# Store order in the start and layernorm of three token chunks inside the last two groups of each cross-attention

## What is computed

```python
def _layernorm(x, axis=-1, eps=1e-05):
    m = jnp.mean(x, axis=axis, keepdims=True)
    v = jnp.var(x, axis=axis, keepdims=True)
    return (x - m) / jnp.sqrt(v + eps)
...
x = x + _L0_xattn_ref(_layernorm(x, axis=-1), ctx_768, ...)
x = x + _L0_ffn_ref(_layernorm(x, axis=-1), ...)
...
x = x + _L3_xattn_ref(_layernorm(x, axis=-1), ctx_768, mask_BxS2_bf1, ...)
x = x + _L3_ffn_ref(_layernorm(x, axis=-1), ...)
```

## Time and profile before

| what | value |
|---|---|
| median of 3 runs | 3842.04 us (3838.91 to 3844.39) |
| profiled execution | 3844.8 us, span 3843.1 us |
| PE busy | 3605.2 us (94%) |
| DVE, ACT, POOL busy | 2533.8, 1933.4, 654.0 us |
| mean granted PE clock | 0.968 of full speed |

### The profile page before, as it was taken

How to read it: one execution, slowest core, us unless ns; L and a number is a source line. 1 busy time by engine, 2 the same in 40 slices (tenths; PEclk the granted TensorE clock), 3 DMA queues, 4 the chain that set the end, 5 groups by cost and what they waited for, 6 DMA issues and landing times. The chain is left out here.

```text
span 3843.1 us, 50411 instructions
## 1 busy us (share of the span) xinstructions
PE 3605.2 (94%) x17554; PEld 1557.4 (41%) x17555; DVE 2533.8 (66%) x5367; ACT 1933.4 (50%) x2358; POOL 654.0 (17%) x946
## 2 busy tenths in 40 slices
PE   5999999799999999987998899999799999998996
PEld 2333333365533333324665333332433333332664
DVE  4888888556678888844223655553478888885523
ACT  2677777621137777772332444445203777777111
POOL 3201000200041000013221301010313001001242
PEclk7999999999999999998999899999899999999998
DMA  6300000123000000015001500000140000001144
GB/s 128 56 19 14 19 14 11 48 76 79 24 26 19 17 16 18 10 37 229 31 30 41 125 18 18 18 18 6 58 94 31 18 18 15 18 11 49 53 121 133
DMA packets 132652, 171.33 MB, mean 45 GB/s; under 512 B 38378, under 2 KB 106588, under 8 KB 130256
## 3 DMA queue, kind: packets, MB, share of 16 engines
q1 hardware_dynamic: 122288, 142.42, 13.4%
q0 software_dynamic: 10144, 26.08, 2.7%
HBM read 131.27 MB, written 40.84 MB: 45 GB/s over the span
## 5 line engine op out<-in xcount | busy, mean ns | idle before, releaser
L1537 DVE TENSOR_REDUCE mx<-ps 128x1 f32<-128x400 f32 (+1 forms) x3584 | 1819.3, 566 | 506.7 <-PE ps L2276 495.4
L1281 ACT ACTIVATE probs<-ps,zero_col 128x1024 f32<-128x1024 f32 (+1 forms) x1040 | 1111.9, 1111 | 579.1 <-PE ps L2315 578.7
L2276 PE MATMUL ps<-k_stack,q_stack 97*128 97x400 bf16 (+1 forms) x3584 | 1077.1, 339 | 50.7 <-DMA k_stack<-k_parts 27.2
L2315 PE MATMUL ps<-q_stack,k_stack 100*128 100x512 bf16 (+2 forms) x3328 | 1056.4, 381 | 6.0 <-ACT probs L1281 6.0
L2329 PE MATMUL ps<-probs,v 128*32 128x512 f32 (+2 forms) x5824 | 892.1, 608 | 0.2 <-ACT probs L1281 0.2
L2276 PEld LDWEIGHTS ps<-k_stack,q_stack 97*128 97x128 bf16 x3584 | 290.7, 97 | 1051.4 <-DVE mx L1537 623.9
L1281 ACT ACTIVATE probs<-ps,mask_col 128x1024 f32<-128x1024 f32 (+1 forms) x416 | 440.0, 1111 | 160.1 <-PE ps L2315 159.9
L2315 PEld LDWEIGHTS ps<-q_stack,k_stack 100*128 100x128 bf16 (+2 forms) x3328 | 323.2, 100 | 344.1 <-ACT probs L1281 65.6
L2329 PEld LDWEIGHTS ps<-probs,v 128*32 128x32 f32 (+2 forms) x5824 | 140.0, 111 | 264.5 <-issue 248.0
L1690 DVE SCALAR_TENSOR_TENSOR x_res<-ps,comb,x_res 128x256 f32<-128x256 f32 x336 | 148.2, 479 | 63.4 <-PE ps L2587 58.2
L1349 ACT ACTIVATE h_t_s<-ps 128x512 f32<-128x512 f32 x80 | 47.8, 597 | 254.6 <-PE ps L2578 254.6
(11 more groups left out here) (298 smaller groups left out, 2770.0 us busy)
## 6 DMA issues: line engine op xcount, KB each, us to landing
q_stack<-q_parts SPq DMA_DIRECT2D x384, 64.0 KB, 2.2
q_parts<-qk_part SPq DMA_DIRECT2D x32, 384.0 KB, 2.5
w_up<-in_up SPq DMA_DIRECT2D x17, 704.0 KB
w_up_s<-in_expert SPq DMA_DIRECT2D x40, 256.0 KB, 2.7
k_stack<-k_parts SPq DMA_DIRECT2D x48, 200.1 KB, 7.4
k_stack<-k_parts POOLq DMA_DIRECT2D x48, 200.1 KB, 4.2
k_parts<-qk_part SPq DMA_DIRECT2D x24, 384.0 KB, 2.9
w_all<-in_up SPq DMA_DIRECT2D x8, 1024.0 KB, 12.6
```

What stands on the lines that cost most here:

```text
L1281: act.activation(PR[pair[0] % 4][0:r, :, :], PS[0:r, 2 * b:2 * b + 2, :], ACT.Exp, bias=mask_col[0:r, k:k + 1] if L == 3 else zero_col[0:r ...
L1537: ins = dve.reduce_max(MX4[g % 2][:, u, c:c + 1], PS[:, bank, 0:CK[c]], AX.X)
L2276: last = mm(PS[:, bank, 0:CK[c]], QS[g][0:97, slot_of(j), qt * P:(qt + 1) * P], KS[0:97, (g * hpg + j) * nsub, CKO[c]:CKO[c] + CK[c]], sta ...
L2315: last = mm(PS[0:r, b + i, :], KS[0:rows, (g * hpg + jj) * nsub + sub, k * P:k * P + r], QS[g][0:rows, slot_of(jj) + sub, :], start=sub == ...
```

## The change

In the start SP's order is another: the second query part is stored right behind the first loads of keys, key parts 4 to 7 are stored between the loads (they stood behind the gate loads), and the second group's keys are loaded last. In every attention's last iteration the `bn_stats` of the first 12 token tiles move from the fourth group to the third, where their variances follow; ACT takes the root of these at the beginning of the fourth group; there DVE inverts at key tile 1 and normalises two token tiles at each of key tiles 7 to 12. `XN` is placed 512 elements lower, so that its first three chunks cover the stacked queries of groups 0 to 2. Behind the fence the last chunk alone is left.

```diff
-            sb("skip_sums", [P, 4 * 2 * Q + 2 * Q + 2 * 64 + 16 + 2 * Q + NG // 2 * Q + Q], f32, ln2)
+            sb("skip_sums", [P, 4 * 2 * Q + 2 * Q + 2 * 64 + 16 + 2 * Q + NG // 2 * Q], f32, ln2)
@@ sync
             load_queries(0, (0, 0), 0)
             load_keys(sp, 0, 0)
+            store_query_parts(0, 1)
             load_value_weights(0)
+            store_key_parts(4)
             load_queries(0, (0, 1), 1)
-            load_keys(sp, 0, 1)
-            store_query_parts(0, 1)
-            wait_landed(qd)
-            load_queries(0, (0, 2), 2)
+            store_key_parts(5)
             sp.dma_start(mask_u8[:, 0:NK - 1], ...
...
             sp.dma_start(mask_row_u8[:], A["mask"]).then_inc(s_mask, 16)
+            wait_landed(qd)
+            load_queries(0, (0, 2), 2)
+            for u in range(6, 8):
+                store_key_parts(u)
+            load_keys(sp, 0, 1)
             for L in range(4):
...
                 if L == 0:
-                    for u in range(4, 8):
-                        store_key_parts(u)
                     wait_landed(kd)
@@ scalar
-                def iteration(first):
+                def iteration(first, last=False):
                     for g in range(NG):
+                        if last and g == NG - 1:
+                            root(0, NT - TPQ)
                         for k in range(NK):
                             exps(k)
...
-                iteration(False)
+                iteration(False, True)
...
-                root()
+                root(NT - TPQ, NT)
                 copy_turned(range(NQ), 0)
@@ vector
+            def normalize_early(g, k):
+                early = NT - TPQ
+                if g == NG - 2:
+                    if k == 0:
+                        dve.wait_ge(s_sf, sf.at())
+                    if k < early:
+                        last = dve.bn_stats(stat[:, k, :], X[:, k, :])
+                        if k == early - 1:
+                            link(last)
+                    else:
+                        variances(0, early)
+                elif k == 1:
+                    deviations(0, early)
+                elif k >= NK - early // 2:
+                    for t in range(early - 2 * (NK - k), early - 2 * (NK - k) + 2):
+                        last = dve.tensor_scalar(XN[:, t, :], X[:, t, :], mv[:, t, 0:1], rstd[:, t:t + 1],
+                                                 ALU.subtract, ALU.mult)
+                    if t % TPQ == TPQ - 1:
+                        last.then_inc(s_xn, 1)
+                        xn.step()
...
             def normalize_tokens(keep):
-                statistics()
-                for c in range(NQ):
-                    normalized(c, [XN[:, c * TPQ + i, :] for i in range(TPQ)])
+                variances(NT - TPQ, NT)
+                deviations(NT - TPQ, NT)
+                normalized(NQ - 1, [XN[:, t, :] for t in range(NT - TPQ, NT)])
...
-                            if last and g == NG - 1 and k < NT - TPQ:
-                                if k == 0:
-                                    dve.wait_ge(s_sf, sf.at())
-                                dve.bn_stats(stat[:, k, :], X[:, k, :])
+                            if last and g >= NG - 2:
+                                normalize_early(g, k)
```

More of the change, by code:

```diff
@@ L1457, in deviations @@
                 link(dve.reciprocal(rstd[:, lo:hi], rstd[:, lo:hi]))
-            def statistics():
-                variances(0, NT)
-                deviations(0, NT)
+            def normalize_early(g, k):
[18 more added lines that the diff above has]
+                        xn.step()
             def shifts():
```

## The result

The changed kernel takes 3822.5 us (median of five runs; 3821.3 to 3825.6) against 3842.04 before (five runs too), a ratio of 0.9951 [0.9939, 0.9963]. Forecast were 3819 and a range of 3810 to 3832. The profiled spans are 3843.1 and 3820.4 us, 22.7 apart, and the sum of the prediction was 22.7. That the two agree to a tenth is luck: the three stretches that were forecast give 19.5 us, in which the cost came out 5.0 us higher than forecast and one gain 3.1 us larger, and the other 3.2 us lie in work that the change doesn't touch.

What follows compares the result with a forecast made beforehand. TensorE, busy in 94% of the span, was taken as the bound. Terms -12.2 + 9.7 - 20.2 = -22.7 us against the profiled 3844.8 gave 3822.1, hence 3819.3 for the median; range 3810 to 3832.

Steps and rivals of the forecast that it cites:

- The start: Before the second chunk's transposes: reordered stores shrink TensorE's stall (8.8 us) and keep its clock (3.4 us), 12.2 us gained.
- some 10 us of issue: SyncE's queue in the start: mask loads, third query set, key parts 6 and 7, second key set, done at about 74.
- the sign named for a mistake: In the start: being right meant no wait of more than 1 us for a store of key parts.
- rival (b): Start gives little: the freed wait returns at the query copies or the late second key set; 3831.5 us, chance 0.15.
- The last groups: Fourth group of each attention: ScalarE's uncovered table loads and root cost about 2.6 us, 2.0 in attention 2; 9.7 lost.
- the fit in the third group: Third group: twelve bn_stats of 0.35 us fit VectorE's idle 0.64 us a tile, costing nothing.
- rival (d): Last group: the pause lowers TensorE's clock and keeps it low; gain gone from 12 us per attention; slower, chance 0.03.
- The heads: Head of the feed-forward, four layers: only the last chunk remains behind the fence; 3.1, 4.6, 9.2 and 3.25 us saved, 20.2.
- T + 7.3: Feed-forward head: gate products begin 7.3 us after T, the start of the aggregation behind the fence, with two chunks at low clock.
- The bound of 26.8: Feed-forward heads: upper bound of the saving, 26.8 us, with all chunks at 2.4 GHz.
- (a): Behind each fence the clock holds: 26.8 us saved in place of 20.2, so 3812.7 us; chance 0.13.
- (c): Last groups: each table switch also costs a 1.38 us drain on ScalarE, 21 us in all, so 3830.6 us; chance 0.06.

Runs made afterwards that it cites:

- filled pause: Changed kernel plus ten unread TensorE products of 512 columns during the table-load pause in attentions 0, 1 and 3: 3819.8 us, ratio 0.9946.
- the start alone: Kernel before with only the new order of SyncE's queue in the start: 3826.9 us, ratio 0.9964.
- two round trips: Changed kernel with a second Exp and Sqrt behind the root, so four table loads stand where two stood: 3836.1 us, ratio 0.9988.
- masks late: Changed kernel with GpSimd's masks behind chunk 1's splits, mask loads behind the second key set, key parts 6 and 7 stored before the third query set: 3824.1 us.
- all three: Changed kernel with the root on VectorE, eight unread products ahead of TensorE's fence, and the edit of masks late: 3806.8 us, ratio 0.9923.

## Why the prediction was right

**The start (12.2 predicted).** Right in size: over the nine executions with this order the first exponential is at 112.1 on average, 12.9 us earlier, and 10.9 in the profile of after is the smallest. The stall shrank from 9.3 to 0.59 as worked out (0.5), and that TensorE keeps its clock over chunk 1's stretch held in all nine (the kernel after lost it behind that, between 75 and 85 us, and alone of the nine). Parts 4 and 5 were stored at 58.4 and 62.4 and the transposes began at 66.4 (59, 65 and 69 were forecast); TensorE came to them 2.8 us sooner too, so that the stall is the one worked out. Part of the lead is not the order's: the mean clock of the window 50 to 60 is 0.56 in before, and from 0.54 to 0.93 in the nine. The four with 0.54 to 0.59, which compare with before, have the first exponential at 112.3 to 113.6, 11.4 to 12.7 us earlier; the earliest, 109.3, goes with the 0.93. What sets that clock is not shown. Wrong was "some 10 us of issue" taken as harmless: the third query set held the stores of key parts 6 and 7, and the sign named for a mistake, a wait of over 1 us for a store of key parts, is there, at 3.3 to 5.1 us in the nine executions with this order. In eight of them the copy of chunk 2's queries waits too, 2.9 to 3.8 us for a store of queries, which is the link that rival (b) named. Both were mostly hidden behind TensorE's maxima and projections (it stood 1.54 us in the kernel after).

**The last groups (9.7 predicted, 14.7 measured).** This is the term that was mis-sized. The statistics at nothing, the fit in the third group and the two loads of 1.28 us were right. The pause itself costs 2.9 us in attentions 0, 1 and 3 and 1.7 in attention 2 (filled pause), 10.5 in all for 9.7; why it is 2.9 and not 2.6 in the three is not shown. The other 4.2 went when the pause was filled and the clock kept: they are rival (d) in small, a fall of the clock that doesn't last. The prediction had set against it that TensorE recovered from longer stalls; it did recover here too, but at 0.50 it could not feed ScalarE (3.4 us in attention 0), and each such stretch cost 1.1 to 1.6. Recovery and cost had been treated as alternatives.

**The heads (20.2 predicted, 23.3 measured).** All four in the window forecast, layer 2 included; T + 7.3 was too late by 0.6 to 0.9. In layer 0 the transposes begin 0.1 us before T and the clock fell only at 719.24 (worked out from the 0.62 of the window 719 to 720), so that the first 0.37 us of them ran at 2.4 GHz, where I had put the first two chunks wholly at 1.2: the first two pairs of copies begin at T + 1.60 and T + 3.30 (720.58 and 722.28) in place of 2.05 and 3.9, and from there on the steps are those of the prediction. In layers 1, 2 and 3 the gate products came 0.2 to 0.3 us earlier still. The bound of 26.8 for all heads at 2.4 GHz is 27.0 by the prediction's own 5.6 us a head, which changes nothing.

**The rivals.** (a) is what ten heads of 36 do by themselves, and in no kernel all four. (b) is excluded by the start alone (12.7 us at the first exponential). (c) is excluded by two round trips.

## What to carry to other kernels

Price a pause on the pacing engine twice: its own length, and what TensorE loses at the lower clock when it comes back (here 2.9 and 1.1 to 1.6 us where the clock fell); both are read in one stretch, not in the total. If a small function needs another table on ScalarE in the middle of its work, count what the same function takes in plain steps on an engine that stands idle: 4.7 us hidden beat 2.8 us exposed by 15 us over four attentions. When a queue's order is mended, look for the next store behind loads that are due much later; the wait moves there.

## What was not expected of the hardware

The granted clock fell in the last group after TensorE had resumed: the pause of 2.35 us ended at 680.49, and the windows show 1.00 from 680 to 681, 0.84 in the next microsecond and 0.50 only from 682. The low stretch thus lies on work that seems far from its cause. And the issue of like DMAs isn't constant in length: the three gate loads took 1.47 us of SyncE's queue in the kernel after (behind six key loads) and 6.33 in masks late and 6.48 in all three, where the mask loads stood between them. The reason is not shown.
